# A graph attention and R-GCN kernel: windows of 192 projected rows for each edge tile instead of 224

## The reference: what is computed

```python
# layer 0: attention over edges and a self loop for each node, 4 heads of 32
xl, xr = x @ Wl, x @ Wr
m = leaky_relu(xl[src] + xr[dst], 0.2)
logits = einsum("ehc,hc->eh", m, att)
alpha = softmax of logits over the edges that share dst
out = segment_sum(alpha * xl[src], dst)      # then graph norm over all nodes, ELU
x = layernorm(x + layer0)
# layer 1: two relational steps, 32 edge types, 4 bases; nodes of the segment sum: 50000
h = tanh(segment_sum(sum_b comp[type, b] * (h[src] @ basis[b]), dst) + h @ loop_w + bias)
x = layernorm(x + h)
```

## Time and profile before

| | us |
|---|---|
| three executions | 3268.5, 3273.53, 3284.71 |
| their median | 3273.53 |
| the profiled execution, its own time | 3273.11 |
| its span, first to last instruction | 3271.3 |
| busy in the span: PE, DVE, ACT, POOL | 2862.2, 2466.4, 1709.4, 1707.3 |
| mean granted TensorE clock, as a share of full speed | 0.957 |

### The profile page before, as it was taken

The page is one execution under the profiler, slowest core; times in us unless marked ns, Lnnn a source line. Parts: engine busy times, 40 slices in busy tenths (PEclk is TensorE's granted clock), DMA queues, the critical chain, the costliest instruction groups (busy, mean ns, idle before and its releaser), DMA issues.

```text
span 3271.3 us, 64645 instructions
## 1 busy us (share of the span) xinstructions
PE 2862.2 (87%) x16643; PEld 2069.6 (63%) x16643; DVE 2466.4 (75%) x7657; ACT 1709.4 (52%) x4118; POOL 1707.3 (52%) x2037
## 2 busy tenths in 40 slices
PE   4898688898857888899799999889989999979897
PEld 4888677777745554788555555468855555536665
DVE  5999677776758889788677777644457777758998
ACT  2555233333323444899666666534446666645565
POOL 1120676676611222577777777512257777745554
PEclk9999799999979999999899999989999999989999
DMA  7999688887848887899433333379943333339997
GB/s 178 272 273 273 175 197 197 198 200 188 194 105 233 240 242 217 259 294 293 151 104 104 104 104 104 91 250 300 303 143 103 104 104 105 103 83 318 334 338 256
DMA packets 754302, 640.70 MB, mean 196 GB/s; under 512 B 75927, under 2 KB 631532, under 8 KB 753932
## 3 DMA queue, kind: packets, MB, share of 16 engines
q1 hardware_dynamic: 573874, 405.72, 43.9%
q0 software_dynamic: 54208, 130.20, 14.4%
q10 hardware_dynamic: 125850, 100.61, 9.9%
HBM read 402.00 MB, written 234.23 MB: 194 GB/s over the span
## 4 chain that ended last, share of the span: by engine, by line
POOL 24%; DVE 17%; DMA 15%; PE 15%; issue 13%; ACT 9%; ACTq 4%; SPq 2%; DVEq 0%; POOLq 0%
POOL work L921 23%; DMA w_d<-work 10%; ACT work L1414 4%; PE bank L1200 4%; PE bank L1207 3%; DMA work<-w_d 2%; DVE work L1727 2%; DVE work L1794 2%; DVE work L1729 2%; DVE self_logit L1731 2%; ACTq L468 2%; PE bank L1001 1%; ACT work L1406 1%; PE bank L1220 1%; PE bank L1174 1%
## 5 line engine op out<-in xcount | busy, mean ns | idle before, releaser
L2053 DVE SCALAR_TENSOR_TENSOR work<-bank,coef,work 128x128 f32<-128x128 f32 x2400 | 674.4, 343 | 241.1 <-ACT work L1448 238.0
L1153 PE MATMUL bank<-basis_s,work 128*128 128x512 f32 x1600 | 756.3, 596 | 1.5 <-ACT work L1441 1.5
L879 POOL DMA_INDIRECT work<-xl_d,slot_src x400 | 398.8, 997 | 249.9 <-issue 191.6
L921 POOL DMA_INDIRECT work<-x_d,slot_src x400 | 382.8, 957 | 126.3 <-issue 121.6
L921 POOL DMA_INDIRECT work<-h_d,slot_src x400 | 382.3, 956 | 123.8 <-issue 121.6
L1448 ACT ACTIVATE work<-bank,coef 128x128 f32<-128x128 f32 x800 | 294.0, 367 | 225.2 <-PE bank L1153 225.2
L1153 PEld LDWEIGHTS bank<-basis_s,work 128*128 128x128 f32 x1600 | 274.6, 191 | 196.9 <-issue 193.1
L1164 PEld LDWEIGHTS bank<-work 128*126 128x126 f32 x1600 | 207.7, 189 | 101.6 <-issue 100.9
L1207 PEld LDWEIGHTS bank<-work 128*128 128x128 f32 x1552 | 206.6, 194 | 97.6 <-issue 92.9
L1001 PE MATMUL bank<-work 112*128 112x125 f32 x1600 | 249.3, 286 | 0.0
L893 POOL DMA_DIRECT2D conv_d<-work x99 | 73.8, 750 | 323.7 <-DVE work L1942 315.0
(11 more groups left out here) (271 smaller groups left out, 6516.3 us busy)
## 6 DMA issues: line engine op xcount, KB each, us to landing
w_d<-work SPq DMA_DIRECT2D x800, 62.5 KB
work<-in_x_dram SPq DMA_DIRECT2D x194, 256.0 KB, 4.1
work<-x_d SPq DMA_DIRECT2D x194, 256.0 KB, 4.5
work<-xr_d SPq DMA_DIRECT2D x400, 112.0 KB
work<-w_d SPq DMA_DIRECT2D x398, 64.0 KB, 3.4
work<-w_d ACTq DMA_DIRECT2D x390, 64.0 KB, 3.4
xl_d<-work SPq DMA_DIRECT2D x97, 256.0 KB, 2.8
xr_d<-work SPq DMA_DIRECT2D x97, 256.0 KB, 3.4
```

What stands on the lines that cost most here:

```text
L879: pool.indirect_dma_start(gathered(i)[:, c, :], None, xl_d, bass.IndirectOffsetOnAxis(ap=slot_src[:, a:a + 1], axis=0)).then_inc(e_in[i % ...
L921: pool.indirect_dma_start(quad(0, i % 3)[:, c, :], None, (x1_d, h1_d)[l], bass.IndirectOffsetOnAxis(ap=slot_src[:, a:a + 1], axis=0)).then ...
L1153: pe.matmul(psum[YBANKS[k % 5]][:, :], quad(1, i % 2)[:, c, :], basis_s[:, l, :, :].rearrange("k b n -> k (b n)"), start=True, stop=True). ...
L2053: ins = dve.scalar_tensor_tensor(o, psum[YBANKS[k % 5]][:, b * D:(b + 1) * D], coef[:, i, l, c, b:b + 1], o, ALU.mult, ALU.add)
```

## The change

One constant is changed. Everything that is worked out from it follows: each of the 400 windows is loaded as 192 rows on 96 partitions, 96 KB instead of 112 KB; the two matrices for a tile have 96 partitions; the products on PE contract over 96 partitions; the limit of the spread of a tile's dst falls from 223 to 191, and the highest start of a window rises from 49776 to 49808.

```diff
--- before.py
+++ after.py
@@ -62,7 +62,7 @@
 TILES_E = CHAINS * ROWS
 GAP = 256
 SLOTS = TE + 1
-WINDOW = 224
+WINDOW = 192
 LANES = WINDOW // 2
 BLOCK = 4
 BLOCKS = ROWS // BLOCK
```

## The result

The kernel with windows of 192 rows takes 3265.24 us (median of 20 executions, 3251.96 to 3277.03), that with 224 rows 3274.49 us in 20 executions beside it. The ratio, taken of the means (3265.62 and 3277.15), is 0.9965, 95% interval 0.9954 to 0.9977: 11.5 us faster, interval 7.5 to 15.1 us; the medians lie 9.2 us apart. (3274.49 is the median of the longer series; three of its executions stand ahead.) That is a gain clear of its interval, though under half a per cent. The forecast was 18 us, 3255, with 3242 to 3277 as the range; 3265 lies in it.

The account below looks back on a forecast made before the run. The edge stretch was taken to be bound by ACT waiting for w_d stores to land. Window loads save 18 us, issue, TensorE and DVE nothing: 3273.1 less 18 gives 3255, range 3242 to 3277.

Parts of the forecast that it names:

- What bounds the stretch: Edge stretch, 343 to 943 us: ACT's L1276 waits 291.9 us for w_d stores to land, in 91 of 100 rows.
- Compute at nothing: Matmuls L1001 and comparisons L1749 on 96 partitions instead of 112 were taken to save 0 us.
- issue at nothing: SP's 400 window DMA issues remain, median 343 ns; fewer lines were taken to save 0 us.
- No fallback: Tiles span at most 159 node numbers, under the limit of 191, so the branch for unsorted edges isn't entered.
- The size, 18 us: Window loads: 0.256 us of engine time saved a row, about midway between 14.4 and 23.3 us on the path.
- The lower end, 14.4 us: Window loads' saving counting only the chain's share in store or window flight: 100 times 0.256 times 0.561.
- branch A: The forecast itself: shorter window loads gain 14 to 23 us, 3250 to 3259; chance 0.46.
- Rival D: Ordinary rows are paced by PE; only the 25 rows with a rel_d load gain, 6 us, 3267; chance 0.12.
- The averaging over 16 engines: Window loads: four times 16 packets saved at 64 ns, spread over 16 DMA engines, 0.256 us a row.
- Rival C: Stores lie on a few engines, full in every row; each row gains 0.256 us, 25.6 us, 3248; chance 0.15.
- Rival B: Windows don't pace the stores, or each engine used keeps eight lines of a window; 0 us, 3273; chance 0.20.
- Rival E: Narrower weights load more slowly on TensorE, 15 ns for 1600 loads, 24 us slower, 3297; chance 0.07.

Follow-up runs that it names:

- load224_use192: Against the kernel of 224 rows: windows still loaded with 224 rows on 112 partitions, compute on 96 partitions; ratio 0.9998 (0.9984 to 1.0012).
- w208: Windows of 208 rows on 104 partitions, against the kernel of 224 rows; ratio 1.0024 (1.0011 to 1.0037), 7.9 us slower.
- w176: Windows of 176 rows on 88 partitions, against the kernel of 224 rows; ratio 1.0017 (1.0000 to 1.0035), 5.6 us slower.
- w160: Windows of 160 rows on 80 partitions, against the kernel of 224 rows; ratio 0.9930 (0.9915 to 0.9946), 22.9 us faster.
- split_224: Windows of 224 rows, each 125-line store sent as two transfers of 112 and 13 lines, against the kernel of 224; ratio 1.0044 (1.0030 to 1.0057), 14 us slower.

## Why the prediction was right, and where its sum was off

- **What bounds the stretch: right.** ACT behind the landing of w_d stores. Shown by the stores of 112 lines: that wait nearly vanishes and 32 us go with it.
- **Compute at nothing, issue at nothing: right.** For the compute, load224_use192 leaves 0.9998. For the issue, the median of L461 stayed at 343 ns.
- **No fallback: right.** Its branch would have shown in hundreds of added transfers; the instruction count is the same 64645.
- **The size, 18 us: too large; 11.5 (7.5 to 15.1) measured.** The price of a window line held: in the trace from 343 to 940 us the 44800 packets of 1024 bytes on q1 took 65.8 ns on average (68.1 for the 38400 after), and I had taken 64. The term that was mis-sized is the share of the saved 25.6 us (0.256 us a row) that lies on the path. I took 18 of 25.6, 70%, midway between the 56% by which the chain was DMA and the 91 rows in which ACT waits; 11.5 of 25.6 is 45%, 29 ns for each of the four lines that an engine is spared in a row. The lower end, 14.4 us, is inside the measured interval, so the step from there to 18 is what failed. A row's wait can shrink by 0.25 us without the row ending 0.25 us sooner; the waits for PE and ACT that grew fit that.
- **The range tests little.** 3242 to 3277 also covers no effect at all (3273). The 11.5 us lie below the 14 to 23 of the forecast's own branch A, between it and D, and inside the 16.4 us that I had called no change, while "faster" had the larger chance, 0.49 against 0.44.
- **The averaging over 16 engines was the wrong model with a nearly right number.** While the loads use all 16, four lines fewer on each engine are four lines fewer on the five that matter as well, so here the mean gave the same number; that was luck. It fails as soon as the divisor changes: by it 208 and 176 would be gains of 6 to 17 us; they are losses.
- **Rival C: the stores do lie on a few engines, but these aren't full in every row.** 25.6 us would have needed each window line to count in full. The stores' own lines do, as near as can be told (32 ns of 32), those of the windows don't (29 of 64). Why a neighbour's line costs less than half is open: rows held by PE would do it, as would packets that overlap on an engine. An estimate from the trace's packets speaks for some overlap: if all stores use the same five engines and the rest is spread evenly, one of the five has 3.3 us of store lines, 1.8 of window lines, 1.3 of gathers and 0.5 of rel_d in a row, 6.9 us in 5.77. No run separates the two.
- **Rival B** (eight lines on each engine before and after) was out: 16 engines both times. But its idea, that lines on the busiest engine count, is what w208 and w176 bear out.
- **Rival D** holds in part. By my own sign for it (the wait for w_d falls and PE or DVE waits rise by the same) the profile after came close. Its time, 6 us for 25 rows, lies below the measured interval, and as a floor it is out by w160. **Rival E** fell, with medians unchanged.
- **What I said the profile would show:** packets and megabytes as said; about 5.6 us a row, 5.70 came, with L1276's first and last start 6.7 us nearer and not 18; the wait for w_d was to fall by about 18 us and fell by 41.8 in this pair, mostly returned elsewhere. Store pieces of 5.1 us didn't come out: the common piece stays near 5.3, and fewer of the chain's microseconds are such pieces.

## What to carry to other kernels

When a kernel waits for one small transfer, count its lines on the fullest DMA engine, not its bytes, and see which partition counts share those engines: here the stores of 125 lines stood on five engines, and 120 lines, more bytes than 115 but on 15 engines, were 18 us faster. Before cutting a transfer, look at the divisors of its partition count: 192 rows (96 partitions) gained, 176 rows (88) lost. And price a spread that needs more issues on every queue that issues them: the spread as two transfers lost 14 us on a full SP; as one, with 13 unneeded lines left out, it gained 32.

## What the runs showed of the hardware that I had not expected

- Loads of 104 partitions on 13 engines made the kernel slower than loads of 112 on 16 (by 7.9 us over 400 loads, 4 to 12), and loads of 88 on 11 by 5.6 us (0 to 11.5), though they move fewer bytes.
- The number of engines of a transfer can be read from the count of packets under 512 B: 1200 and 2000 fewer with 13 and 11 engines, 4000 more with 15 instead of five. In split_224 it is 9600 more, 24 for each store (16 and 13 for the two pieces, less the five before).
- Estimates from the ratios: a line of a waiting store cost 32 ns on the path (22 to 43), about all of its own time, a line of a load beside it 29 ns (19 to 38) of 64.
- Chips differ by more than the change: the same kernel had medians of 3264 to 3291 us.
